# The last half step of an embedding-interaction kernel: a second late tile copied by ACT, ACT's other work given to VectorE, and late tiles taken one by one

## The reference

```python
x = relu(dense @ Wb0 + bb0); x = relu(x @ Wb1 + bb1)
d = relu(x @ Wb2 + bb2)                      # 2048 x 64
sp = emb[arange(26)[None, :], sparse_idx]    # 2048 x 26 x 64, gathered
T = concatenate([sp, d[:, None, :]], axis=1) # 27 vectors of 64 per sample
Z = einsum('bnd,bmd->bnm', T, T)             # all pair products
h = concatenate([d, Z[:, li, lj]], axis=1)   # lower triangle: 351 pairs
h = relu(h @ Wt0 + bt0); h = relu(h @ Wt1 + bt1)
p = sigmoid(h @ Wt2 + bt2)
```

## Time and profile before

| what | value |
|---|---|
| median of three executions | 521.33 us (520.81 to 522.19) |
| the profiled execution's own time | 520.35 us |
| its span, first to last instruction | 518.6 us |
| POOL busy | 378.7 us, 73% of the span |
| PE busy | 310.7 us, 60% |
| DVE busy | 244.2 us, 47% |
| ACT busy | 14.0 us, 3% |
| mean granted TensorE clock | 0.737 of full speed |

### The profile page before, as it was taken

How to read it: one execution, slowest core, us unless ns; L and a number is a source line. 1 busy time by engine, 2 the same in 40 slices (tenths; PEclk the granted TensorE clock), 3 DMA queues, 4 the chain that set the end, 5 groups by cost and what they waited for, 6 DMA issues and landing times.

```text
span 518.6 us, 12247 instructions
## 1 busy us (share of the span) xinstructions
PE 310.7 (60%) x3388; PEld 226.8 (44%) x3388; DVE 244.2 (47%) x373; ACT 14.0 (3%) x26; POOL 378.7 (73%) x406
## 2 busy tenths in 40 slices
PE   3799983754374355534456625555536373589897
PEld 1233333642373334424246423444426362377765
DVE  6444766772464335633257324462445434433122
ACT  1000000000000000000000000000000000012211
POOL 5777777777777777777777777777777777777760
PEclk9987897885677766857667675685756775569699
DMA  6444323333243332444324443354333444332320
GB/s 212 33 28 29 28 31 28 28 30 28 30 29 28 27 29 29 29 27 29 28 28 28 29 27 29 28 30 27 28 30 27 28 29 27 28 28 28 30 28 3
DMA packets 20187, 16.86 MB, mean 33 GB/s; under 512 B 11923, under 2 KB 13212, under 8 KB 20121
## 3 DMA queue, kind: packets, MB, share of 16 engines
q0 software_dynamic: 12768, 13.10, 31.6%
q1 hardware_dynamic: 4634, 2.72, 3.5%
q10 hardware_dynamic: 2732, 0.51, 2.4%
HBM read 16.28 MB, written 0.01 MB: 31 GB/s over the span
## 4 chain that ended last, share of the span: by engine, by line
POOL 72%; issue 23%; PE 2%; DMA 1%; DVE 1%; POOLq 0%; ACT 0%; ACTq 0%; DVEq 0%
POOL rows L370 71%; POOL rows L399 1%; DMA rows<-in_emb,idx_row 1%; DMA idx_raw<-in_idx 1%; PE ps_t L606 0%; PE ps_t L558 0%; PE ps_gram L523 0%; PE ps_feat L558 0%; POOLq L122 0%; DVE gram_s L882 0%; POOLq L366 0%; PE ps_turn L471 0%; ACT feat L728 0%; ACT vecs_st L722 0%; DVE gram_s L884 0%
## 5 line engine op out<-in xcount | busy, mean ns | idle before, releaser
L370 POOL DMA_INDIRECT rows<-in_emb,idx_row x392 | 370.4, 945 | 122.4 <-issue 119.4
L438 PE MATMUL ps_turn<-ident,rows 128*128 128x128 f32 x182 | 40.8, 365 | 143.7 <-DMA rows<-in_emb,idx_row 135.1
L857 DVE COPY vecs_st<-ps_turn 128x512 f32<-128x512 f32 (+1 forms) x49 | 47.0, 959 | 111.8 <-PE ps_turn L438 111.3
L857 DVE COPY vecs_mv<-ps_turn 64x512 f32<-64x512 f32 (+1 forms) x98 | 96.2, 981 | 0.7
L438 PEld LDWEIGHTS ps_turn<-ident,rows 128*128 128x128 f32 x182 | 27.1, 183 | 158.4 <-issue 150.0
L487 PE MATMUL ps_gram<-vecs_mv,vecs_st 128*32 128x54 f32 x1792 | 41.7, 271 | 29.2 <-DVE vecs_mv L857 15.4
L487 PEld LDWEIGHTS ps_gram<-vecs_mv,vecs_st 128*32 128x32 f32 x1792 | 37.4, 152 | 34.9 <-DVE vecs_mv L857 18.2
L606 PE MATMUL ps_t<-wt_sb,ht_t 128*128 128x256 f32 x128 | 51.2, 570 | 0.0
L606 PEld LDWEIGHTS ps_t<-wt_sb,ht_t 128*128 128x128 f32 x128 | 35.0, 287 | 15.1 <-issue 8.1
L882 DVE STREAM_TRANSPOSE gram_s<-ps_gram 128x864 f32<-128x864 f32 x16 | 17.3, 1083 | 46.2 <-PE ps_gram L487 39.7
L585 PE MATMUL ps_t<-feat_t,wt_sb 117*128 117x128 f32 x180 | 35.0, 349 | 0.2 <-ACT feat_t L750 0.2
(11 more groups left out here) (82 smaller groups left out, 241.1 us busy)
## 6 DMA issues: line engine op xcount, KB each, us to landing
fetched<-in_emb SPq DMA_DIRECT2D x1024, 0.2 KB
fetched<-in_emb ACTq DMA_DIRECT2D x1024, 0.2 KB
rows<-in_emb,idx_row POOLq DMA_INDIRECT x399, 3.5
rows<-in_emb SPq DMA_DIRECT2D x128, 0.2 KB
wt_sb<-in_wt SPq DMA_DIRECT2D x1, 1024.0 KB
wb_sb<-in_wb SPq DMA_DIRECT2D x1, 512.0 KB
wt_sb<-in_wt SPq DMA_DIRECT2D x1, 512.0 KB
idx_raw<-in_idx SPq DMA_DIRECT2D x1, 179.0 KB, 2.8
```

What stands on the lines that cost most here:

```text
L370: nc.gpsimd.indirect_dma_start(rows[:, t, h * DIM:(h + 1) * DIM], None, emb_rows, bass.IndirectOffsetOnAxis(idx_row[:, c:c + 1], 0)).then_ ...
L438: turned = nc.tensor.transpose(ps_turn[r % 2][:, j, :], rows[:, first + j, :], ident[:, :])
L857: moved = nc.vector.tensor_copy(to, source)
```

## The change

Six things are changed, and all of them act in the last step.

1. Both tiles of quarter 2 are now copied by plain DMAs: k = 0 by SP as before, k = 1 by ACT, 128 DMAs in four blocks behind its part of the last table's rows. POOL gathers six late tiles, quarter 3's directly behind quarter 1's.
2. Until its 128 DMAs are issued ACT does nothing else. All that it did in the last step before the late tiles (`spread_last` of even k, `place_d_last`, `copy_d_last`, `relu_top`, `pack(i, 0)`, `move_feat(i, 0)`) goes to DVE.
3. Each late tile is turned and spread alone: even ones by ACT, odd ones by DVE.
4. PE turns tile 6 before `gram_quarter(2)`, and tile 7 in the middle of it; one `stay_busy(1)` falls away.
5. The second transposition of the products (416 columns) is split in 160 and 256 columns. Each pair tile is packed, turned and moved by itself, with semaphores of its own: packing by ACT, DVE, ACT, moving by DVE, ACT, DVE.
6. `top_0_last` starts when tile 0 has been moved.

The core of the diff:

```diff
-COPIED_Q, COPIED_K = 2, 0
-LATE_RUNS = [(q, 0, LATE_TILES) for q in range(QUARTERS - 1)] + [(QUARTERS - 1, k, 1) for k in range(LATE_TILES)]
+TILE_DELTAS = (0, (PAIR_ROWS + VECS - 1) // VECS, (2 * PAIR_ROWS + VECS - 1) // VECS, DELTAS)
+COPIED_Q = 2
+LATE_RUNS = [(q, k) for q in range(QUARTERS) for k in range(LATE_TILES)]
...
+        turned_tiles = [bank[0:PAIR_ROWS, 0, :] for bank in (ps_feat[1], ps_turn[0], ps_turn[1])]
+        def unrolled_last(k):
+            lo, hi = TILE_DELTAS[k:k + 2]
...
# POOL
-            for l, (q, tile, n) in enumerate(LATE_RUNS):
-                for k in range(tile, tile + n):
-                    if (q, k) == (COPIED_Q, COPIED_K):
-                        continue
+            for l, (q, k) in enumerate(LATE_RUNS):
+                if q != COPIED_Q:
...
# PE
+            def wait_spread(k):
+                if k < LAST_NR:
+                    pe.wait_ge(vecs_dve, (STEPS - 1) * NR + k + 1)
+                elif k % 2 == 0:
+                    pe.wait_ge(vecs_act, (k - LAST_NR) // 2 + 1)
+                else:
+                    pe.wait_ge(vecs_dve, (STEPS - 1) * NR + LAST_NR + (k - LAST_NR) // 2 + 1)
...
             def turn_late(l):
...
                 if q == COPIED_Q:
-                    pe.wait_ge(late_landed[l], 16 * (n - 1))
-                    pe.wait_ge(late_fetch_landed, 16 * P)
+                    pe.wait_ge(late_fetch_landed[tile], 16 * P)
                 else:
-                    pe.wait_ge(late_landed[l], 16 * n)
...
+                    pe.wait_ge(late_landed[l], 16)
+                wait_spread(k - 2)
+                nc.tensor.transpose(ps_turn[k % 2][:, 0, :], late_rows(q, tile), ident[:, :]).then_inc(rows_turned, 1)
...
             def turn_feat_last():
+                pe.wait_ge(first_tile_packed, 1)
+                nc.tensor.transpose(turned_tiles[0], feat[:, 1, 0:PAIR_ROWS], ident[:, :]).then_inc(first_tile_turned, 1)
                 pe.wait_ge(feat_packed, STEPS * 2)
...
                 turn_late(0)
+                turn_late(1)
                 stay_busy(1)
                 gram_quarter(0)
                 stay_busy(1)
-                turn_late(1)
+                turn_late(2)
+                turn_late(3)
                 stay_busy(1)
                 gram_quarter(1)
-                turn_late(2)
+                turn_late(4)
+                turn_late(5)
                 stay_busy(1)
-                gram_quarter(2)
-                turn_late(3)
-                turn_late(4)
-                stay_busy(1)
+                turn_late(6)
+                gram_quarter(2, 0, 4)
+                turn_late(7)
+                gram_quarter(2, 4, 8)
                 gram_quarter(3)
                 stay_busy(4)
                 turn_feat_last()
+                pe.wait_ge(first_tile_moved, 1)
+                for m in range(T0 // P):
+                    top_0_last(0, m)
                 pe.wait_ge(feat_moved, STEPS * 2)
...
# ACT
-                spread_last(0)
-                place_d_last()
-                relu_top(i - 1, 0)
-                spread_last(2)
-                relu_top(i - 1, 1)
-                spread_last(4)
-                copy_d_last()
-                spread_last(6)
-                pack(i, 0)
-                move_feat(i, 0)
-                spread_last(8)
-                relu_top(i, 0)
-                spread_last(10)
                 spread_late(0)
                 spread_late(2)
                 spread_late(4)
+                spread_late(6)
                 pack_last()
                 move_feat_last()
                 relu_top(i, 1, top_0_blocks_last(0))
...
-            act.wait_ge(d_ready, CHUNKS)
-            act.wait_ge(pads_ready, 3)
+            act.wait_ge(rows_turned, STEPS * NR)
+            for jj in range(4):
+                places = load_places(mybir.EngineType.Activation, 1, jj, STEPS)
+                for j in range(PART):
+                    act.dma_start(late_landing(1, jj * PART + j), emb_bytes[bass.ds(places[j], ROW_BYTES)])\
+                        .then_inc(late_fetch_landed[1], 16)
             last_step()
...
# DVE
+            def turn_gram_last():
+                dve.wait_ge(gram_summed, STEPS * 2)
+                wrapped = gram_s[1][:, VECS * SLOTS:WRAP * SLOTS]
+                n = TILE_DELTAS[1]
+                nc.vector.transpose(gram_s[1][:, 0:VECS * SLOTS], unit_products(VECS)).then_inc(gram_turned, 1)
+                nc.vector.transpose(wrapped[:, 0:n * SLOTS], unit_products(n)).then_inc(gram_turned, 1)
+                nc.vector.transpose(wrapped[:, n * SLOTS:], unit_products(DELTAS)[:, n:]).then_inc(rest_turned, 1)
...
+                spread_last(0)
+                place_d_last()
+                relu_low(i - 1, 0)
+                relu_high(i - 1, 0)
                 spread_last(1)
-                relu_high(i - 1, 0)
+                spread_last(2)
                 logit(i - 1, 0)
+                relu_low(i - 1, 1)
+                relu_high(i - 1, 1)
                 spread_last(3)
-                relu_high(i - 1, 1)
+                spread_last(4)
                 logit(i - 1, 1)
+                copy_d_last()
                 move_fetched(i)
                 spread_last(5)
+                spread_last(6)
                 turn_gram(i, 0)
+                pack(i, 0)
                 spread_last(7)
+                move_feat(i, 0)
+                spread_last(8)
+                relu_low(i, 0)
                 spread_last(9)
                 relu_high(i, 0)
+                spread_last(10)
                 logit(i, 0)
                 spread_last(11)
                 spread_late(1)
                 spread_late(3)
-                turn_gram(i, 1)
+                spread_late(5)
+                spread_late(7)
+                turn_gram_last()
                 pack_last()
                 move_feat_last()
```

More of the change, by code:

```diff
@@ L457, in turn_late @@
             def turn_late(l):
-                q, tile, n = LATE_RUNS[l]
+                q, tile = LATE_RUNS[l]
                 k = LAST_NR + l
                 if q == COPIED_Q:
-                    pe.wait_ge(late_landed[l], 16 * (n - 1))
-                    pe.wait_ge(late_fetch_landed, 16 * P)
-                else:
-                    pe.wait_ge(late_landed[l], 16 * n)
-                if k % 2 == 0:
-                    pe.wait_ge(vecs_act, k // 2)
-                else:
-                    pe.wait_ge(vecs_dve, (STEPS - 1) * NR + k // 2)
-                for j in range(n):
-                    turned = nc.tensor.transpose(ps_turn[k % 2][:, j, :], late_rows(q, tile + j), ident[:, :])
-                turned.then_inc(rows_turned, 1)
+                    pe.wait_ge(late_fetch_landed[tile], 16 * P)
+                else:
+                    pe.wait_ge(late_landed[l], 16)
+                wait_spread(k - 2)
+                nc.tensor.transpose(ps_turn[k % 2][:, 0, :], late_rows(q, tile), ident[:, :]).then_inc(rows_turned, 1)
             def gram(i, u):
@@ L707, in _ @@
         def _(act):
-            def place_d_last():
-                for h in range(2):
-                    placed = nc.scalar.activation(vecs_st[DIM * h:DIM * (h + 1), :, DSLOT],
-                                                  d_all[:, bass.ds((STEPS - 1) * STEP + h * P, P)], ACT.Copy)
-                placed.then_inc(d_placed, 1)
-            def spread_last(k):
-                act.wait_ge(rows_turned, STEPS * NR + k + 1)
-                nc.scalar.activation(*turned_half(k), ACT.Copy).then_inc(vecs_act, 1)
```

111 lines of the change are left out of this document (50 added, 61 removed).

## The result

Six executions of the kernel after took 525.22 to 529.45 us, median **526.96 us**; six of the kernel before, on the same chip, took 520.81 to 522.19 us, median 521.34 us. The ratio is 1.0104, with a 95% interval of 1.0075 to 1.0132. The kernel is **slower**, by 5.4 us by the ratio and 5.6 us by the medians. The forecast was 522.6 us and no change, in a range up to 525.0 us; the result lies above that range. The profiled execution took 525.22 us with a span of 523.5 us, so it stands 1.7 us under the median. Its span is 4.9 us longer than before's.

A forecast was written before the change was run, and what follows sets the result against it. POOL's row of gathers sets the pace, and the end hangs on the last landings and PE's order. ACT free late +0.87, copies late +1.15, tail -0.72 give +1.3 us: 522.6 us, no change, range 520.5 to 525.0.

The forecast's parts named there:

- When the copies land: ACT's last copy, issued at 501.8, lands after 5.0 us (ends 1.5 and 7.1); tile 5's turning waits, 1.15 us more.
- ACT's work on VectorE: Last step: work moved to DVE starts half 0's gram about 0.9 us later, hidden behind ACT, so no cost.
- The cover: ACT being busy until 502.0 lets turn_last(11), at 498.02 before, come 0.9 or even 2 us later without touching gram 0.
- The gather that goes: POOL's last late gather starts at 501.74 instead of 502.99; worth 1.25 us only if nothing else is late.
- ACT free late: ACT issues DMAs until 502.0, so gram 0 starts at 502.5 and the last gram ends 0.87 us later.
- Copies late: Tile 5 is there at 506.8 but PE needs it at 505.65, so the last gram ends 1.15 us later.
- From gram 0 to G: From quarter 0's gram, at 502.5, to the end of the last gram, near 509.6, with the wait for tile 5.
- The tail: Behind the last gram, top_0 starts after 2.56 us instead of 3.28, a gain of 0.72 us.
- (1): Copies hold up turn_late(5) and tile 4 just before it; at 7.1 us landing +3.4 us, 524.7 us; chance 0.27.
- (2): Copies land within 4 us, so only ACT's lateness and the tail count: +0.15 us, 521.5 us; chance 0.15.
- (3): ACT isn't the bound: its issues end before 502.0 or PE's order absorbs them; -1.65 us, 519.7 us; chance 0.09.
- (4): Clock falls as PE idles before gram 0 and tile 5; tail costs up to 4.4 us more, 525.7 to 527; chance 0.07.

The follow-up runs named there:

- the gathered version: The changed kernel without ACT's 128 copies in the last step, tile 5 gathered by POOL again: 520.95 us against 522.09 us for the kernel before, ratio 0.9975.

## Why the prediction was wrong

**The step that failed** is the sentence at the end of "When the copies land": that POOL's gathers beside the copies "have more room", 4.7 us for quarter 1's second and up to 508 for quarter 3's. Their landing was never put into the sum as a term, and quarter 0's second tile, on which it fell, isn't in that sentence at all. It measured 8.0 us in the median and 6.3 at the least, where the median is over the 7.1 us that I had as the *highest* of any row. Quarter 0's second tile started at 496.74, had 5.8 us until the forecast start of gram 0 at 502.5, and took 8.17. I had read rows 11 and 12 rightly (a second stream makes everything late), but carried them over to the copies alone.

The same omission stands in "ACT's work on VectorE". I expected landings between 455 and 495 "well over 3.5 us", and gave them no cost. PE waited 1.69 us for them ahead of half 0's gram. The cover, by which `turn_last(11)` may come "even 2 us" later than 498.02, was too thin: it ran at 501.82, 3.8 us later. Of that lateness 1.9 us are waits for landings (1.69 + 0.21); the rest isn't shown to be the copies'.

And I took the maximum in 410 to 449 as an upper end, though one of `keep_pace`'s longer pauses lies in that window (SP from 433.3 to 438.6), while the last step has only the short ones. A longer look at the kernel before would have warned me: in its landing events a group's last share came 8.8 us behind its last gather's start at 346.9, near the end of seven blocks in a row on both queues (SP's from 261.2 to 349.1).

Term by term:

- **The gather that goes**: right. The last one starts at 501.73; forecast 501.74.
- **ACT free late, +0.87 us**: wrong, and without weight. ACT was free at 500.53 and not at 502.0, since its blocks began at 450.25 and not 451.8 (the 50.2 us of issuing was right), and it then waited 3.3 us for PE. Whether 500.53 alone would have cost something against a gram 0 that is ready at S + 5.18 = 500.67 wasn't tried. An estimate from 500.53 and 0.37 us for the spreading is 0.2 to 0.3 us.
- **Copies late, +1.15 us**: they landed at 507.64, 7.3 us after issue, over my 5.0 and over my upper end of 7.1. But PE needed them only at 510.02, because everything ahead of them was late as well. The term was 0.
- **From gram 0 to G**: forecast 502.5 to 509.6, 7.1 us; measured 505.84 to 513.09, 7.25 us. The agreement is chance: mine was 5.95 us of work and 1.15 us of waiting for tile 5, the real one 6.11 us of work and 1.14 us for the clock.
- **The tail, -0.72 us**: right; 0.64 us, the same in each of the four versions with the new tail whose chain is shown.
- **ACT's work on VectorE, 0**: right within tenths. In the gathered version it shows as 0.25 us ahead of half 0's gram and a wait of 0.32 us ahead of tile 1's turning, and that version is still quicker than the kernel before.

Mended, the sum is the forecast's +1.3, and 3.34 us more because gram 0 started at 505.84 and not at 502.5, 0.15 us more from there to G, and 0.08 us more for the tail: +4.87 us, as the spans say.

**The rivals.** (1) "The copies are late enough to cost" named the cause, an over-full stream with 7 us to land, but at the wrong place, turn_late(5), and so too small: 524.7 us. (2), the copies landing within 4 us, fell: they took 7.3. Of (3) the condition came true, as ACT's issues ended at 500.53 and ACT wasn't the bound, but its time did not, because the landings held gram 0. (Its sum is also 0.1 us off: 500.6 and the forecast's 5.95 us to G give 506.55, not 506.65.) (4), the clock, did happen, for 3.4 us behind a wait and not in the tail: 1.14 us and not 4.4.

**The rule I weighed and what it left out.** The trace shows that copies and gathers get into each other's way, and that only one share in 16 of a gather is late. The Trainium skill, page "DMA: Bandwidth & Descriptors", section "Why a DMA increments its semaphore by 16 and not by 1", says that a DMA's number of engines follows from the sizes of its slowest dimension and can be one, that SP's and ACT's path takes the lowest-numbered engines, and that 128 partitions are spread over all 16. By that rule all 256 copies, each one element of 256 bytes, would meet on the same engine, which holds one sixteenth of each gather. The trace agrees in that one landing event of 16 is late; it doesn't name the engine, so that it is the same one isn't shown. The prediction had cited, from the same page of the Trainium skill, section "Issuing engines are not separate DMA queues", that a second issuer saves only its own issue time. That saving came (POOL's last gather starts 1.26 us earlier, at 501.73), and the landings cost more than it gave.

## What to carry to other kernels

Small copies on two queues at once can be issued faster than they land (here one per 0.32 us and one per 0.41 us on SP's queue), and then one share of every gather waits with them. Read the *maximum* landing time of the other transfers, over the longest stretch without a pause, and ask whether the pauses that kept it low remain. If a transfer is moved to another issuer, the landing of the transfers left behind is a term of the sum, with the same range as that of the moved one. A wait of a microsecond in front of short matmuls can be paid twice, if the granted clock falls behind it. And where a chain hands a long landing to one transfer, look at how long the engine really stood idle for it: here 1.14 us of 8.17.

## What the runs showed of the hardware that I had not expected

- **A backlog grows with both streams and drains with longer pauses.** Gathers landed in 2.5 us (median) with SP's copies alone at the end of the kernel before, in 8.0 us behind 50 us of both streams, and in up to 21.7 us where both ran without `keep_pace`; there it stopped growing at 20 to 22 us. The median over a long stretch hardly moved (3.6 to 3.8 us with both streams), because gathers share semaphores; only the maximum told.
- **One share of 16 is late**: in the six late gathers it came 3.8 to 6.0 us behind the fifteenth, and the others were as quick as before.
- **Chips of two kinds.** Seven of the groups of runs were on chips where the same kernel takes 857 to 870 us, some 1.65 times as long, with POOL's gathers no slower each (944 ns) and the chain in SP's issuing; on the others it takes 521 to 522 us. What differs there wasn't tried. On a usual chip ACT's copies cost over 5 us; on the others the version without them stood 0.0 to 0.4% under the kernel before, and the one without SP's copies some 26 us under it. So one has to see which kind a run was on before reading it.
